# Four graph layers on one core: the first attention pass finishes its nodes itself, source lists are loaded two steps ahead, and the last layer becomes one stage

## What is computed

```python
x = _layernorm(x + _L0_gnn_ref(...))   # attention, 4 heads, edge features; inside: y = ln(out + bias + x) * gamma + beta; relu
x = _layernorm(x + _L1_gnn_ref(...))   # relational: 8 bases, 64 edge types
x = _layernorm(x + _L2_gnn_ref(...))   # two transformer convolutions, 8 heads and 1 head
x = _layernorm(x + _L3_gnn_ref(...))   # two GCN convolutions

def _gcn_conv(x, W, b, src, dst, n):
    h = x @ W
    deg = segment_sum(ones, d)                       # with a self-loop for each node
    norm = rsqrt(deg)[s] * rsqrt(deg)[d]
    return segment_sum(norm[:, None] * h[s], d) + b
```

## Time and profile before

| | us |
|---|---|
| time, median of 3 runs (4648.46 to 4659.68) | 4654.02 |
| the profiled execution | 4652.1 |
| its span, first to last instruction | 4650.3 |
| PE busy | 2810.4 (60%) |
| DVE busy | 3001.2 (65%) |
| POOL busy | 2727.2 (59%) |
| ACT busy | 934.8 (20%) |
| transfers: 526.18 MB | 113 GB/s over the span |

### The profile page before, as it was taken

One profiled execution on the slowest core, in us unless ns is written; L12 is line 12 of the kernel. 1 busy time (PEld: TensorE's weight loads), 2 busy tenths in 40 slices (PEclk: granted clock), 3 DMA queues, 4 the chain that ended last, 5 costly groups with the idle time before them and its releaser, 6 DMA issues. The chain is left out here.

```text
span 4650.3 us, 56109 instructions
## 1 busy us (share of the span) xinstructions
PE 2810.4 (60%) x18074; PEld 2599.7 (56%) x18075; DVE 3001.2 (65%) x6284; ACT 934.8 (20%) x781; POOL 2727.2 (59%) x2656
## 2 busy tenths in 40 slices
PE   1356656656614555556566456666666667994955
PEld 0356656656613555555556356655665657983744
DVE  6355655655676666676665477777777778996144
ACT  0121221211201222222221121221221123441000
POOL 0577777777705777777773277777777723551000
PEclk9566656656656677776668767777777779996977
DMA  1444444444404455445443356556655625540532
GB/s 20 109 98 110 102 99 109 100 102 109 98 21 103 134 135 136 136 132 136 135 133 90 84 138 154 147 146 153 153 144 149 153 56 123 115 106 1 171 95 92
DMA packets 169458, 526.18 MB, mean 113 GB/s; under 512 B 60851, under 2 KB 87800, under 8 KB 156470
## 3 DMA queue, kind: packets, MB, share of 16 engines
q1 hardware_dynamic: 74032, 299.78, 26.1%
q0 software_dynamic: 95264, 224.28, 18.6%
HBM read 456.40 MB, written 67.48 MB: 113 GB/s over the span
## 5 line engine op out<-in xcount | busy, mean ns | idle before, releaser
L544 POOL DMA_INDIRECT e0G<-table,e0src x858 | 851.9, 993 | 439.1 <-issue 405.1
L544 POOL DMA_INDIRECT e21G<-table,e21src x858 | 856.1, 998 | 408.1 <-issue 257.6
L1364 POOL DMA_INDIRECT t1G<-table,t1idx x806 | 789.7, 980 | 375.5 <-issue 242.0
L1437 PE MATMUL t1psW<-t1CO,t1G 128*128 128x192 f32 x1612 | 435.9, 434 | 303.9 <-issue 285.6
L1437 PEld LDWEIGHTS t1psW<-t1CO,t1G 128*128 128x128 f32 x1612 | 370.4, 258 | 312.2 <-issue 292.2
L568 PE MATMUL e21psQ<-Q,e21OT 121*128 x1716 | 412.5, 410 | 129.6 <-DVE e21G L682 54.3
L568 PEld LDWEIGHTS e21psQ<-Q,e21OT 121*128 121x128 f32 x1716 | 399.8, 326 | 141.4 <-issue 81.6
L561 PE MATMUL e0psQ<-Q,e0OT 121*128 x1716 | 398.7, 371 | 94.3 <-ACT e0OT L599 58.2
L561 PEld LDWEIGHTS e0psQ<-Q,e0OT 121*128 121x128 f32 x1716 | 396.6, 325 | 99.8 <-issue 99.8
L2103 POOL TENSOR_TENSOR e22Z<-e22Z,e22C 121x847 f32<-121x847 f32 (+1 forms) x104 | 200.1, 1955 | 259.0 <-ACT e22Z L2095 259.0
L584 PE MATMUL e21psA<-e21G,e21O 128*121 128x145 f32 x1716 | 272.4, 330 | 106.1 <-DVE e21G L733 106.1
(11 more groups left out here) (428 smaller groups left out, 5250.8 us busy)
## 6 DMA issues: line engine op xcount, KB each, us to landing
e0dstb<-in_dst_p SPq DMA_DIRECT2D x27, 1996.5 KB
e21dstb<-in_dst_p SPq DMA_DIRECT2D x27, 1996.5 KB
e22C<-counts SPq DMA_DIRECT2D x26, 1487.0 KB
Q<-in_type_p SPq DMA_DIRECT2D x62, 416.0 KB
counts<-X SPq DMA_DIRECT2D x13, 1487.0 KB
planes<-SKIP SPq DMA_DIRECT2D x26, 743.5 KB
counts<-RES SPq DMA_DIRECT2D x13, 1487.0 KB
e31C<-planes SPq DMA_DIRECT2D x26, 743.5 KB
```

What stands on the lines that cost most here:

```text
L544: nc.gpsimd.indirect_dma_start(out=G[:, u, t, 0:width], out_offset=None, in_=table, in_offset=bass.IndirectOffsetOnAxis(ap=src[:, u, t:t + ...
L1364: nc.gpsimd.indirect_dma_start(out=G[:, q % 2, t, :], out_offset=None, in_=table, in_offset=bass.IndirectOffsetOnAxis(ap=idx[:, q * GT + t ...
L1437: mmi = nc.tensor.matmul(psW[:, k % 2, 0:WIN * NBAS], G[:, q % 2, t, :], CO[:, k % 2, i].rearrange("p b w -> p (b w)"), start=(i == 0), st ...
```

## The change

- **Sources.** The source lists of steps 0 and 1 are the first loads of the attention pass (both passes). In the loop SP loads the edges of step s + 1 first, then waits for the scores of step s and loads the sources of step s + 2.
- **Finish in the pass.** In e0 DVE calls `finish_block` at the end of each step in place of the copy into RES: the arithmetic of `gat_finish` on one block (39 instructions), with one Exp and three square roots on ACT. ACT stores the finished block into the table of the relation stage. `gat_finish` and p1 go.
- **Last layer.** After p31 one stage `last_layer` does both sweeps. In the first sweep PE, after the sums of a block, waits for their end, then turns the block before and multiplies the block before that with the second weights; DVE scales and splits into HP2 four blocks at a time. In the second sweep DVE normalises block pairs as they come and SP stores each pair, between the loads of planes.

The diff, cut:

```diff
+        rows_table=tab[128]
         attention_pass(g, "e0", tab[132], 132, 4, True)
-        gat_finish(g)
-        project(g, "p1", [], tab[128], "copy")
         relation_tiles(g, "t1", tab[128], tab[256])
...
-            for c in (1, 2):
-                project(g, f"p3{c}", [(f"L3_gnn_W{c}", None)], tab[128], "gcn", source=X if c == 1 else RES)
-                dense_sum(g, f"e3{c}")
-                gcn_finish(g, f"f3{c}", f"L3_gnn_b{c}", out if c == 2 else None)
+            project(g, "p31", [("L3_gnn_W1", None)], tab[128], "gcn")
+            last_layer(g, out)

 # attention_pass, SP
+            for u in range(2):
+                e = sp.value_load(g["steps_i"][0:1, SMAX + u:SMAX + u + 1], min_val=0, max_val=E)
+                load_edges(sp, a, src[:, u, :], "src_p", e, sources_in[u])
...
-                    sp.wait_ge(S["scores_made"], s + 1)
-                    sp.sem_inc(S["waited"], 1)
-                    load_edges(sp, a, src[:, u, :], "src_p", e, sources_in[u])
                     sp.wait_ge(S["edges_used"], s + 1)
                     sp.wait_ge(S["targets_ready"], s + 1)
                     sp.sem_inc(S["waited"], 1)
                     for buf, what in bufs:
                         load_edges(sp, a, buf[:] if what != "attr_p" else buf, what, e2, S["edges_in"])
+                    sp.wait_ge(S["scores_made"], s + 1)
+                    sp.sem_inc(S["waited"], 1)
+                    load_edges(sp, a, src[:, u, :], "src_p", e, sources_in[u])   # e: step s + 2

 # attention_pass, ACT, end of a step
+                    if gat:
+                        act.wait_ge(S["exp_wanted"], s + 1)
+                        nc.scalar.activation(fe[:], fs[:, 0:8], ACT.Exp).then_inc(S["exp_made"], 1)
+                        for k, x in enumerate((fc, fv, fv)):
+                            act.wait_ge(S["root_wanted"], s * 3 + (k + 1))
+                            nc.scalar.activation(x[:], x[:], ACT.Sqrt).then_inc(S["rooted"], 1)
+                        blk = act.value_load(g["steps_i"][0:1, bass.ds(s, 1)], min_val=0, max_val=NB - 1)
+                        act.wait_ge(S["row_ready"], s + 1)
+                        act.wait_ge(row_stored[1 - u], i * 16 + (16 + 16 * u))
+                        act.dma_start(rows_table block blk, xo[:, u, :]).then_inc(row_stored[u], 16)

 # attention_pass, DVE, end of a step
+            def finish_block(s, i, u, blk):
...
+                V.tensor_tensor(fs[:, 4:8], al, m, ALU.subtract).then_inc(S["exp_wanted"], 1)
+                dve.wait_ge(S["rooted"], s * 3 + 1)
+                V.reciprocal(g["cnt1"][:, bass.ds(blk, 1)], fc[:])
+                dve.wait_ge(S["exp_made"], s + 1)
...
+                norm(fy[:], s, 2)
...
+                norm(fy[:], s, 3)
+                dve.wait_ge(row_stored[u], i * 16 + 16)
+                V.tensor_scalar(xo[:, u, :], fy[:], fv[:], None, ALU.mult).then_inc(S["row_ready"], 1)
...
-                    V.tensor_copy(RES[:, bass.ds(blk, 1), 0:NC].rearrange("p a f -> p (a f)"), ST[:])
+                    if gat:
+                        finish_block(s, i, u, blk)

+def last_layer(g, out):
...
+        def _(sp):
+            sp.dma_start(w2[:], a["L3_gnn_W2"]).then_inc(S["consts"], 16)
+            for i in range(2):
+                sp.dma_start(bias[:, i, :], a[f"L3_gnn_b{i + 1}"].partition_broadcast(BN)).then_inc(S["consts"], 16)
+            with sp.Fori(0, n) as k:
+                for b in range(NB):
+                    load(b, k, k * NB + b)
+            with sp.Fori(0, n) as k:
+                for b in range(NB):
+                    load(b, k, n * NB + k * NB + b)
+                    if b % 2 == 1 and b >= RING:
+                        store(k, b // 2 - RING // 2)
...
+        def _(pe):
+                for b in range(NB + 2):
+                    if b < NB:
+                        pe.wait_ge(counts_in[b % RING], k * 32 + (b // RING * 16 + 16))
+                        pe.wait_ge(S["taken"], k * NB + (b + 1))
+                        sums(b, HP, S["summed"])
+                        pe.wait_ge(S["summed"], k * NB + (b + 1))
+                        pe.sem_inc(S["buffer_free"], 1)
+                    if 1 <= b <= NB:
+                        turn(b - 1, k)
+                    if b >= 2:
+                        make(b - 2, k)
...
+                    if b == 0:
+                        pe.wait_ge(S["parts_ready"], n * NGRP)
+                    sums(b, HP2, S["summed2"])
+                    pe.wait_ge(S["summed2"], k * NB + (b + 1))
+                    pe.sem_inc(S["buffer_free"], 1)
...
+        def _(dve):
+            def take(b, made, count, taken, acc):
+                dve.wait_ge(made, count)
+                V.tensor_reduce(part[:, b % 2], ps[0:BN, b % 2, 0:3 * D]..., AX.X, ALU.add).then_inc(taken, 1)
+                V.tensor_tensor(acc, acc, part[:, b % 2], ALU.add)
...
+                    if b % 2 == 0 and i >= 1:
+                        norm_end(i - 1, k)
+                    if b % 2 == 1:
+                        norm_start(i, k)
+                norm_end(NB // 2 - 1, k)
```

More of the change, by code:

```diff
@@ L495, in attention_pass @@
             pr = sb("pr", [128, T, 13])
+            aff = sb("aff", [BN, 3, D])
+            fs = sb("fs", [BN, 20])
+            fe = sb("fe", [BN, 8])
+            fy = sb("fy", [BN, D])
+            ft = sb("ft", [BN, D])
+            fm = sb("fm", [BN, 1])
+            fv = sb("fv", [BN, 1])
+            fc = sb("fc", [BN, 1])
+            xo = sb("xo", [BN, 2, D])
         psQ = ctx.enter_context(nc.psum_tensor(name + "psQ", [128, 3, 512], F32))
@@ L501, in attention_pass @@
                  "ends_turned", "carry_ready", "carry_turned", "diff_ready", "weights_done", "values_ready",
-                 "sums_done", "sums_free", "merge_ready", "merge_done", "pe_waited", "consts", "squared", "one_set")
+                 "sums_done", "sums_free", "merge_ready", "merge_done", "pe_waited", "consts", "squared", "one_set", "act_waited", "exp_wanted", "exp_made", "root_wanted", "rooted", "row_ready")
         S = {n: sem(n) for n in names}
         gathered = [[sem(f"gathered{u}{b}") for b in range(NG)] for u in range(2)]
+        row_stored = [sem(f"row_stored{u}") for u in range(2)] if gat else None
         sources_in = [sem(f"sources_in{u}") for u in range(2)]
@@ L513, in _ @@
                 sp.dma_start(atte[:], a["L0_gnn_att_edge"].rearrange("h c -> (h c)").partition_broadcast(128)).then_inc(S["consts"], 16)
+                for i, n in enumerate(("L0_gnn_bias", "L0_gnn_ln_gamma", "L0_gnn_ln_beta")):
+                    sp.dma_start(aff[:, i, :], a[n].partition_broadcast(BN)).then_inc(S["consts"], 16)
             bufs = [(dst3, "dst_p"), (dstb, "dst_all")]
@@ L533, in _ @@
                         load_edges(sp, a, buf[:] if what != "attr_p" else buf, what, e2, S["edges_in"])
+                    sp.wait_ge(S["scores_made"], s + 1)
+                    sp.sem_inc(S["waited"], 1)
+                    load_edges(sp, a, src[:, u, :], "src_p", e, sources_in[u])
+            pairs = g["n_pairs"](sp)
+            for u in range(2):
+                sp.wait_ge(sources_in[u], pairs * 16 + 16)
+                sp.sem_inc(S["waited"], 1)
         @block.gpsimd
@@ L611, in _ @@
                     nc.scalar.activation(ex[:], mm[:, 0:2 * H], ACT.Exp).then_inc(S["merge_done"], 1)
+                    if gat:
[7 more added lines that the diff above has]
+                        act.wait_ge(row_stored[1 - u], i * 16 + (16 + 16 * u))
+                        act.sem_inc(S["act_waited"], 1)
+                        act.dma_start(g["rows_table"].rearrange("(b p) f -> b p f", p=BN)[bass.ds(blk, 1)].rearrange("a p f -> (a p) f"),
+                                      xo[:, u, :]).then_inc(row_stored[u], 16)
+            if gat:
+                pairs = g["n_pairs"](act)
+                for u in range(2):
+                    act.wait_ge(row_stored[u], pairs * 16 + 16)
+                    act.sem_inc(S["act_waited"], 1)
         @block.vector
@@ L616, in bc, with norm @@
                 return x.broadcast_to(shape)
+            def norm(x, s, count):
+                dr = dve.drain
+                V.tensor_reduce(fm[:], x, AX.X, ALU.add)
+                dr()
+                V.tensor_scalar(fm[:], fm[:], 1.0 / D, None, ALU.mult)
+                dr()
+                V.tensor_scalar(x, x, fm[:], None, ALU.subtract)
+                dr()
+                V.tensor_tensor(ft[:], x, x, ALU.mult)
+                dr()
+                V.tensor_reduce(fv[:], ft[:], AX.X, ALU.add)
+                dr()
+                V.tensor_scalar(fv[:], fv[:], 1.0 / D, EPS, ALU.mult, ALU.add).then_inc(S["root_wanted"], 1)
+                dve.wait_ge(S["rooted"], s * 3 + count)
+                V.reciprocal(fv[:], fv[:])
+                dr()
@@ L618, in _ @@
             V = nc.vector
             if gat:
-                dve.wait_ge(S["consts"], 32)
+                dve.wait_ge(S["consts"], 80)
```

(8 more changed lines are left out.)

209 lines of the change are left out of this document (207 added, 2 removed).

## The result

The changed kernel takes 4521.6 us (median of 4; 4515.1 to 4525.9) against 4653.1 for the kernel before beside it: a ratio of 0.9715, 95% interval 0.9698 to 0.9732. That is 131 us less where 172 were forecast: inside the range, 40 us short of the forecast itself. The profiled execution took 4525.9 us, its span is 4524.1.

What follows compares the result with a forecast made beforehand. POOL's gathers and late lists set the first pass, with DVE-only holes behind it and around the plane sums; DVE would become its bound. Terms -16 (second pass), -90 (first pass and finish), -66 (last layer) gave 4482 us, range 4443 to 4530.

Steps and rivals of the forecast that it cites:

- e21: Second attention pass, bound by POOL: 13.9 us from the earlier start and 2.5 from lists, -16 us.
- the 90 us in the first pass: Relation stage starts at 1328.1 instead of 1418.2, nearly all from the finish and the copy of the table.
- The first step: DVE's first step of the first attention pass, claimed to start at 181.2, with POOL starting 16.9 us earlier.
- The finish: Finish instructions added to each DVE step of the first pass: 13.5 us, bounds 11.9 or less to 15.5.
- the third wait: DVE's wait in the finish while ACT goes from Exp to Sqrt: two round trips and the table load, 1.9 us.
- the way round the loop: DVE's gap between steps of the first pass: 1.04 us at loop end, 0.57 inside; 0.9 a step charged.
- The last layer: Last layer as one stage with both plane sweeps: -66 us, bounds -50 to -80.
- the self-wait: PE waiting for its own block's end in the last layer; first sweep 1.1 us a block, bounds 0.1 to 1.2.
- The turn costs more than the load: Rival: in the finish the first Sqrt waits another 1.28 us; step 45.3, +33 us, 4515; chance 0.2.
- The finish fits: Rival: finish under 11.9 us, POOL stays the first pass's bound at 42.5 us a step; 4443; chance 0.15.
- the early list doesn't start the pass: Rival: later edge lists set the first step, both pass starts stay where they were; +31 us, 4513; chance 0.05.
- Slower: Rival: self-waits and small products drop PE's clock in the last layer; +219 us, 4701; chance 0.04.

Runs made afterwards that it cites:

- e3: The kernel before with the new order of loads alone, old finish and old last layer: 4597.3 us, ratio 0.9877.
- e1: The changed kernel with DVE's loop of the first pass announcing its jump back at the top of every turn: 4494.6 us, ratio 0.9660.
- e7: The changed kernel with the last layer's plane buffers released by the counted sums, so PE doesn't wait for its own block: 4491.4 us, ratio 0.9653.
- e8: The changed kernel with finish once for two steps, jump announced, no PE wait for itself, and DVE's first match cut into nine: 4442.2 us, ratio 0.9545.
- e2: The changed kernel with DVE's loop of the first pass written out as 13 pairs of steps, no jump left: 4486.4 us, ratio 0.9638.
- e4: The kernel before with the new last layer alone: 4588.5 us, ratio 0.9861.
- e6: The changed kernel with Exp in place of the finish's three Sqrt, so ACT never changes its function table: 4481.7 us, ratio 0.9631.

## Why the prediction was right, and where it was not

**The order of loads.** POOL's first gather came at 134.38 (forecast 134.7), the list waits went, e21 gave about -15 (-16). But I wrote that nearly all of the 90 us in the first pass was the finish and the copy of the table. e3 shows the opposite: the loads alone give 41 of the 51. My own terms said so (16.9 us of start and 29.4 of lists), and I didn't take them apart: against a pass bound by POOL with early lists, a finish that makes DVE the bound must first earn back what it adds to every step. By those terms the finish was worth 90 - 46 = 44 us; it is 42 with the jump announced (e3 against e1) and 10 without.

**The first step** was forecast at 181.2 and came at 185.99. POOL's 33rd gather was issued at 179.92, 45.5 us after the first, and the score add waited 6.1 us more for its landing; before it waited 2.6. Gathers issued from 160 to 190 us took a median of 7.0 us to land, over the pass 2.6. What lies beside them are the 2 MB of the next step's edges, issued at 167.16 instead of 158.93, because the first edges came 8 us later behind the sources and constants (ACT starts on them at 158.71, before at 150.52). I had named the edges' delay and put it at nothing. That they are the cause fits the times. In all eight kernels with the early lists the first step comes 18.8 to 19.7 us after these edges are issued, from 164.65 and 183.76 in e3 (without the finish's three constant loads) to 168.93 and 188.09 in e7. In e8 the 33rd gather was issued at 178.50, earlier than anywhere else, and didn't bring the first step forward. A run that moves the edges alone was not made.

**The finish**: 13.5 us forecast, 13.0 to 13.6 measured; the third wait 1.9 and 1.88. Adding up operation by operation at the pitches of the earlier trace rows was good to half a microsecond.

**The step that failed** is the 0.9 us a step for the way round the loop, taken from the earlier trace rows, where e21's loop end cost 1.04. It measured 0.87 inside the body and 4.0 at the loop's end, 2.4 on average: 36 us over the pass. The row was of a shorter loop, of 268 instructions. The change added 148 instructions to a loop of 250, and I priced each of them as work on DVE and none as code to be loaded. With the jump announced (e1) the steps are 44.2 us apart, where the forecast said 44.0, and with the loop written out (e2) 44.0. That the range still held the result is luck as to the cause: its upper end stood for a dear turn with a last layer 15 us short, but the turn came at its plain price.

**The last layer**: -66 forecast; -60 between the two profiles, -64 in e4. The stage was to last 275.4 us from its first sum and lasted 278.4. First sweep 5.1 us a block (5.3), chain 8.2 us (6), second sweep 4.8 (4.6), tail 8.6 (9.8). The bounds for the self-wait (0.1 to 1.2) held; it is about 0.6 in both sweeps, and I had taken too much of it in the first and too little in the second. The second sweep also has a slow first block, which I had put at nothing though the old first block stood in my own rows at 3.2 us more: after the chain, with PE busy 2.04 of 8.2 us, the granted clock was 0.59 in that block (between the two levels, 1.2 and 2.4 GHz), and its 26 matmuls took 7.42 us where those of the next took 4.41 (in the timeline).

```profile
4387.61 7.42 PE L2343 MATMUL llps<-llHP,llC 121*121 121x384 bf16 x26 [5.23 <-DVE llHP L2428]
...
4395.43 4.41 PE L2343 MATMUL llps<-llHP,llC 121*121 121x384 bf16 x26 [0.40 <-PE llps L2343]
```

The remaining 3 us lie ahead of the first sum: PE waited 17.8 us for the first plane, 13.7 before, and of these 4.1 us more the forecast had 1.2.

**The rivals.** *The turn costs more than the load* would have given 4515, nearly the measured time, and by another cause: the wait for the root is 1.88 us, and e6 gains what the load alone allows. A time that agrees with a rival is no proof of it; the step of 45.4 us looks like its 45.3 until one sees where in the step the wait is. *The finish fits* is out, as DVE is the bound; *the early list doesn't start the pass* is out by POOL's 134.38. *Slower* is out: the granted clock was 0.98 over both sweeps.

## What to carry to other kernels

Count a loop's instructions before adding to it, and look at the DMA's instruction packets: DVE's loop, once it loaded its code anew each turn, paid some 3 us at the jump back while DVE was the bound, and announcing the jump took most of it away. When a change moves work from its own stage into a pipelined loop, price the loop as it would be with the change's other parts alone, because the gain is against that, and ask which engine's work the added time lies beside. PE, which waited for its own result to release a buffer, paid more than the idle time that the list of waits shows; where it can, let the engine that reuses the buffer count the result instead.

## What the runs showed of the hardware

DVE's loops of 250 and 268 instructions ran a whole pass on 2 or 3 packets of code; 342 and 398 took 62 and 63, about 5 packets of 8 KB a turn, and 3.1 us more at each jump back (4.0 against 0.9). 343 and 399 with the jump announced took 3. The Trainium skill (Runtime: NRT & Kernel Launch, "Instruction fetch mechanics") says that a taken branch to code outside the current window has to wait for its load; the trace agrees in that code packets come while DVE stands at the jump, with 3.1 us beside it. A gather on POOL took 4.84 us instead of 0.94 while one DVE operation of 4.26 us ran, and at most 1.42 when the same match was cut into nine.
